# Attention value products with V's two parts in one operand, and row sums by adding DMAs, in a fused adaLN block

## The reference, cut to what matters

```python
h = layernorm(x) * (1 + cb) + sb
nx = rmsnorm(h, g1)
Q = (nx @ Wq.T).reshape(B, S, 4, 64).transpose(0, 2, 1, 3)
Kc, Vc = nx @ Wkc.T, nx @ Wvc.T                 # 64 features, one set for the 4 heads
scores = einsum('bhsd,btd->bhst', Q, Kc) / 8
out = einsum('bhst,btd->bhsd', softmax(scores), Vc)
X = h + out.transpose(0, 2, 1, 3).reshape(B, S, 256) @ Wo.T
...                                             # a shared and 8 routed experts, top 2, added to X
x = x + gb * (X + moe_out)
```

## Time and profile before

| | us |
|---|---|
| median of three runs (lowest, highest) | 1460.32 (1458.84, 1464.45) |
| profiled execution | 1461.01 |
| its span, first to last instruction | 1459.0 |
| front / loop / tail, in the span | 0 to 235 / 235 to 1114 / 1114 to 1459 |

### The profile page before, as it was taken

One profiled execution on the slowest core, in us unless ns is written; L12 is line 12 of the kernel. 1 busy time (PEld: TensorE's weight loads), 2 busy tenths in 40 slices (PEclk: granted clock), 3 DMA queues, 4 the chain that ended last, 5 costly groups with the idle time before them and its releaser, 6 DMA issues.

```text
span 1459.0 us, 19334 instructions
## 1 busy us (share of the span) xinstructions
PE 1307.4 (90%) x6008; PEld 920.7 (63%) x6008; DVE 1079.0 (74%) x2143; ACT 893.1 (61%) x1450; POOL 385.4 (26%) x282
## 2 busy tenths in 40 slices
PE   4777677999999999999998999999997999999994
PEld 2334545665666665676665666666664797887774
DVE  4956987777887777777885877787974867546778
ACT  2355564776766766666686766666675856555551
POOL 0443431222311212211111311111154001623346
PEclk9989797999999999999999999999998999999998
DMA  5001016200000000000000001000011323555634
GB/s 196 1 1 44 15 58 208 81 1 1 1 1 1 1 1 1 1 1 1 1 1 1 1 1 44 1 0 1 22 51 65 104 93 117 195 148 165 191 115 149
DMA packets 56418, 75.82 MB, mean 52 GB/s; under 512 B 8383, under 2 KB 48063, under 8 KB 56064
## 3 DMA queue, kind: packets, MB, share of 16 engines
q1 hardware_dynamic: 36030, 46.29, 9.7%
q0 software_dynamic: 6144, 16.79, 3.7%
q10 hardware_dynamic: 14146, 11.52, 2.3%
HBM read 37.27 MB, written 37.22 MB: 51 GB/s over the span
## 4 chain that ended last, share of the span: by engine, by line
PE 63%; DVE 19%; issue 5%; ACT 5%; POOL 5%; DMA 1%; ACTq 1%; POOLq 0%; DVEq 0%; SPq 0%
PE PS L1802 8%; PE PS L1700 6%; PE PS L1749 6%; PE PS L1732 6%; PE PS L1751 6%; PE PS L1735 6%; PE PS L1750 6%; DVE mx L1159 5%; PE PS L1828 4%; DVE PL L1189 4%; PE PS L1713 3%; POOL y L1534 2%; PE PS L1686 2%; POOL xbuf L1522 2%; PE PS L1786 1%
## 5 line engine op out<-in xcount | busy, mean ns | idle before, releaser
L1159 DVE TENSOR_REDUCE mx<-PS 128x1 f32<-128x512 f32 x512 | 344.1, 686 | 100.6 <-PE PS L1700 98.5
L770 ACT ACTIVATE PT<-PS 128x1024 f32<-128x1024 f32 x256 | 262.8, 1027 | 231.8 <-PE PS L1735 221.8
L1514 POOL TENSOR_TENSOR PL<-PT,PH 128x1024 fp32r<-128x1024 f32 x61 | 146.2, 2396 | 541.8 <-ACT PH L775 530.1
L775 ACT ACTIVATE PH<-PT 128x1024 fp32r<-128x1024 f32 x256 | 271.2, 1060 | 8.1
L1189 DVE TENSOR_TENSOR PL<-PT,PH 128x1024 fp32r<-128x1024 f32 x195 | 238.9, 1225 | 44.4 <-ACT PH L775 43.8
L1749 PE MATMUL PS<-PH,VH 128*65 128x512 f32 x512 | 219.6, 429 | 8.6 <-DVE PL L1189 8.6
L1751 PE MATMUL PS<-PL,VH 128*65 128x512 f32 x512 | 202.9, 396 | 0.0
L1750 PE MATMUL PS<-PH,VL 128*65 128x512 f32 x512 | 202.3, 395 | 0.0
L1700 PE MATMUL PS<-KA,Q 128*128 128x512 f32 x384 | 161.1, 432 | 16.9 <-DVE mx L1159 12.1
L1732 PE MATMUL PS<-Q,KA 128*128 128x512 f32 x384 | 128.0, 415 | 2.5 <-POOL KB L1491 2.5
L1735 PE MATMUL PS<-Q,KB 65*128 65x512 f32 x384 | 122.6, 401 | 0.0
(11 more groups left out here) (239 smaller groups left out, 2486.5 us busy)
## 6 DMA issues: line engine op xcount, KB each, us to landing
xbuf<-xT SPq DMA_DIRECT2D x26, 384.0 KB, 4.4
xg<-xbuf SPq DMA_DIRECT2D x78, 128.0 KB, 2.3
ybuf<-yo ACTq DMA_DIRECT2D x78, 128.0 KB
nxT<-in_wexp SPq DMA_DIRECT2D x9, 768.0 KB, 4.4
x<-in_x SPq DMA_DIRECT2D x8, 512.0 KB, 11.9
x_scratch<-x SPq DMA_DIRECT2D x2, 2048.0 KB, 6.9
nxT<-x_scratch SPq DMA_DIRECT2D x32, 128.0 KB
out<-X SPq DMA_DIRECT2D x32, 128.0 KB, 1.9
```

The lines of the kernel that those rows point to most:

```text
L770: act.activation(PT[:, gs % 2, :], PS[:, bk:bk + 2, :].rearrange("p a n -> p (a n)"), ACT.Exp, scale=0.125).then_inc(sem("pt"), 1)
L775: act.activation(PH[:, gs % 3, :], PT[:, gs % 2, :], ACT.Copy).then_inc(sem("pt_h"), 1)
L1159: dve.tensor_reduce(mx[:, half, i, c:c + 1], PS[:, k, :], AX, ALU.max).then_inc(sem("dve_out"), 1)
L1514: pool.tensor_tensor(PL[:, gs % 3, :], PT[:, gs % 2, :], phf[:, gs % 3, :], ALU.subtract).then_inc(sem("pl_g"), 1)
```

## The change

V's high and low part become one tile V of 2 x 64 columns. `av` makes two matmuls for each 512 queries: V (128 columns) x PH, which puts high and low part on rows 0 to 63 and 64 to 127 of the bank, and V's high part x PL on rows 0 to 63. woa has Wo on both halves of the partitions (two loads), so the projection adds the halves; it is 128x256 now. All low parts are made by VectorE.

The sum of the exponentials no longer goes through TensorE with the values. For each 1024 queries (a group g of 16 steps) two 128x1024 buffers lie in DRAM. The PT of the first two steps is written to them by SP; those of the other 14 are added by DMAs from GpSimd (`accum_op`), even steps to one buffer, odd steps to the other, each after the one before on its buffer has landed. PT has three slots, and `exp(gs)` also waits until the transfer of gs - 3 has landed. PL has two slots. When a group is through, SP reads both buffers back for 512 queries at a time (Z, 128 x 2 x 512, one slot), `z_mm` sums Z over keys with a column of ones, and VectorE takes four reciprocals at once. O holds 1024 queries only, so the projections of a head's first half are done within the head.

In the diff the first `total` and `z_mm` are SP's, the second `total` is GpSimd's (at the start of each step), the second `z_mm` TensorE's.

```diff
+        todo += spread(z_jobs(bh, 0), 61, 71) + spread(proj_jobs(bh, 0), 62, 93)
         if bh > 0:
-            m, e = (30, 60) if bh == 4 else (49, 92)
-            todo += spread(proj_jobs(bh - 1)[:8], 4, m) + spread(proj_jobs(bh - 1)[8:], m + 1, e)
+            todo += spread(z_jobs(bh - 1, 1), 13, 23) + spread(proj_jobs(bh - 1, 1), 14, 46)
...
-    last = [x for j, p in enumerate(proj_jobs(7)) for x in (p, norm[j])] + [norm[NT]]
-    side = [(-2, 9, last),
-            (2, 2, [j for ex in range(NE) for j in split_jobs(ex)]),
-            (2, 2.5, rlog_jobs(1)),
-            (22, 1, route_jobs(1, 5) + scatter_jobs(1)),
+    proj = proj_jobs(7, 1)
+    last = norm[:8] + [("z_mm", 7, 1, 0)] + proj[:4] + [("z_mm", 7, 1, 1)] + proj[4:] + norm[8:]
+    side = [(0, 9, last),
+            (4, 2.5, [j for ex in range(NE) for j in split_jobs(ex)]),
+            (4, 2.5, rlog_jobs(1)),
+            (25, 1.25, route_jobs(1, 5) + scatter_jobs(1)),
...
+    def summed(w, gs):
+        g, kc = divmod(gs, 16)
+        if kc < 2:
+            w.wait_ge(sem(f"d_zw{kc}"), 16 * (g + 1))
+        else:
+            w.wait_ge(sem(f"d_za{kc % 2}"), 16 * (7 * g + kc // 2))
...
+        def total(gs):
+            g, kc = divmod(gs, 16)
+            if kc < 2:
+                w.wait_ge(sem("pt"), gs + 1)
+                sp.dma_start(zbuf[g, kc], PT[:, gs % 3, :]).then_inc(sem(f"d_zw{kc}"), 16)
+
+        def z_mm(bh, qc, h):
+            g = 2 * bh + qc
+            if g or h:
+                pe_of(w, ("z_mm", *((bh, qc, 0) if h else (*divmod(g - 1, 2), 1)), 0))
+            for a in range(2):
+                summed(w, 16 * g + 14 + a)
+            sp.dma_start(Z[:, :, :], zbuf[g, :, :, h * 512:h * 512 + 512].rearrange("a p n -> p a n")).then_inc(
+                sem("d_z"), 32)
...
             for n in range(NTI // 3):
                 sp.dma_start(zv[n], bc(zero, 3, 1)).then_inc(sem("d_zero"), 16)
         for gs in range(NGS):
+            total(gs)
...
-            if gs >= 2:
-                low_done(w, gs - 2)
-            act.activation(PT[:, gs % 2, :], PS[:, bk:bk + 2, :].rearrange("p a n -> p (a n)"), ACT.Exp,
+            if gs >= 3:
+                w.wait_ge(sem("pl"), gs - 2)
+                summed(w, gs - 3)
+            act.activation(PT[:, gs % 3, :], PS[:, bk:bk + 2, :].rearrange("p a n -> p (a n)"), ACT.Exp,
...
-            act.activation(O[:, q0:q0 + 512], PS[0:65, 4 + n, :], ACT.Copy).then_inc(sem("o"), 1)
+            act.activation(O[:, n * 512:n * 512 + 512], PS[:, 4 + n, :], ACT.Copy).then_inc(sem("o"), 1)
...
+            dve.reciprocal(rz[:, qc, 4 * h:4 * h + 4], PS[:, k, 0:4]).then_inc(sem("dve_out"), 1)
...
-            mark(dve.reciprocal(rz[:, s, :], PS[:, k, 256:257]))
...
-            if gs >= 3:
-                w.wait_ge(sem("av"), 2 * (gs - 2))
-            dve.tensor_tensor(PL[:, gs % 3, :], PT[:, gs % 2, :], phf[:, gs % 3, :], ALU.subtract).then_inc(sem("pl_v"), 1)
+            if gs >= 2:
+                w.wait_ge(sem("av"), 2 * (gs - 1))
+            dve.tensor_tensor(PL[:, gs % 2, :], PT[:, gs % 3, :], phf[:, gs % 3, :], ALU.subtract).then_inc(sem("pl"), 1)
...
-            if not by_pool(gs):
-                low(gs)
+            low(gs)
...
-            pool.tensor_tensor(PL[:, gs % 3, :], PT[:, gs % 2, :], phf[:, gs % 3, :], ALU.subtract).then_inc(sem("pl_g"), 1)
+        def total(gs):
+            g, kc = divmod(gs, 16)
+            if kc < 2:
+                return
+            w.wait_ge(sem("pt"), gs + 1)
+            summed(w, gs - 2)
+            pool.dma_start(zbuf[g, kc % 2], PT[:, gs % 3, :], accum_op=ALU.add).then_inc(sem(f"d_za{kc % 2}"), 16)
...
+        def z_mm(bh, qc, h):
+            w.wait_ge(sem("ones"), 1)
+            w.wait_ge(sem("d_z"), 32 * (4 * bh + 2 * qc + h + 1))
+            k = bank("z_mm", bh, qc, h, 0)
+            for i in range(4):
+                for a in range(2):
+                    mm = pe.matmul(PS[:, k, i:i + 1], Z[:, a, i * P:i * P + P], ones[:, :], start=(a == 0), stop=(a == 1))
...
-            pe.matmul(PS[0:65, 4 + n, :], VH[:, t, :], PH[:, r, c], start=(kc == 0), stop=False)
-            pe.matmul(PS[0:65, 4 + n, :], VL[:, t, :], PH[:, r, c], start=False, stop=False)
-            pe.matmul(PS[0:65, 4 + n, :], VH[:, t, :], PL[:, r, c], start=False, stop=(kc == 15)).then_inc(sem("av"), 1)
+            if kc < 15:
+                pe.matmul(PS[:, 4 + n, :], V[:, t, :, :].rearrange("p a d -> p (a d)"), PH[:, gs % 3, c], start=(kc == 0),
+                          stop=False)
+                pe.matmul(PS[0:64, 4 + n, :], V[:, t, 0, :], PL[:, gs % 2, c], start=False, stop=False).then_inc(sem("av"), 1)
```

More of the change, by code:

```diff
@@ L127, in q_jobs, with proj_jobs, z_jobs @@
     return [(n, b, pair, c) for c in range(4) for n in ("q_mm", "q_hi", "q_lo")]
-def proj_jobs(bh):
-    return [("proj", bh, i) for i in range(NT)]
+def proj_jobs(bh, qc):
+    return [("proj", bh, 8 * qc + i) for i in range(8)]
+def z_jobs(bh, qc):
+    return [("z_mm", bh, qc, h) for h in range(2)]
 def norm_jobs(b):
@@ L231, in tail_order @@
     return {s: flat(v) for s, v in order.items()}
-def by_pool(gs):
-    return gs % POOL_EVERY == POOL_EVERY - 1 and gs < 7 * NSTEP + 20
-def lows(gs, pool):
-    return sum(by_pool(g) == pool for g in range(gs + 1))
 class Once:
@@ L290, in _build @@
     xbuf = [nc.dram_tensor(f"xbuf{b}", [NTI * P, D], F32, kind="Internal").ap() for b in range(NB)]
+    zbuf = nc.dram_tensor("z_scratch", [16, 2, P, 1024], F32, kind="Internal").ap()
     ybuf = [nc.dram_tensor(f"ybuf{b}", [NTI * P, D], F32, kind="Internal").ap() for b in range(NB)]
@@ L346, in _build @@
     mT = sb("mT", [8, 2, P], F32R, c=c3)
-    rz = sb("rz", [P, 2, 1], c=c3)
+    rz = sb("rz", [P, 2, 8], c=c3)
+    ones = sb("ones", [P, 1], c=c3)
     wk = sb("wk", [P, 2, P], c=c3)
@@ L394, in _build @@
     KB1 = sb("KB1", [P, S], F32R, c=c3)
-    PT = sb("PT", [P, 2, 1024], c=c3)
+    PT = sb("PT", [P, 3, 1024], c=c3)
     PH = sb("PH", [P, 3, 1024], F32R, c=c3)
-    PL = sb("PL", [P, 3, 1024], F32R, c=c3)
-    O = sb("O", [65, S], c=c3)
-    woa = sb("woa", [65, 4, 257], c=c3)
+    PL = sb("PL", [P, 2, 1024], F32R, c=c3)
+    Z = sb("Z", [P, 2, 512], c=c3)
+    O = sb("O", [P, 1024], c=c3)
+    woa = sb("woa", [P, 4, D], c=c3)
     QA = [Q01[0][:, :], Q01[1][:, :], QA2[:, :]]
@@ L616, in _ @@
         work = {"spill": spill, "max_turn": max_turn, "load_w": load_w, "split_down": split_down, "gather": gather,
-                "finish": finish}
+                "z_mm": z_mm, "finish": finish}
         run(work, FRONT)
         front_done(w)
-        sp.dma_start(woa[:, :, :], I["woA"]).then_inc(sem("d_woa"), 16)
+        for a in (0, 64):
+            sp.dma_start(woa[a:a + 64, :, :], I["woA"][0:64, :, 0:D]).then_inc(sem("d_woa"), 16)
         w.wait_ge(sem("zero"), 1)
@@ L774, in exp @@
                 w.wait_ge(sem("av"), 2 * (gs - 2))
-            act.activation(PH[:, gs % 3, :], PT[:, gs % 2, :], ACT.Copy).then_inc(sem("pt_h"), 1)
+            act.activation(PH[:, gs % 3, :], PT[:, gs % 3, :], ACT.Copy).then_inc(sem("pt_h"), 1)
         def o_out(gs, n):
@@ L1556, in _ @@
         for gs in range(NGS):
-            if by_pool(gs):
-                low(gs)
+            total(gs)
             for part in range(3):
@@ L1709, in proj, with z_mm @@
             qc, n = divmod(i, 8)
-            w.wait_ge(sem("d_woa"), 16)
+            w.wait_ge(sem("d_woa"), 32)
+            q0 = n * P
             w.wait_ge(sem("o"), 4 * bh + 2 * qc + n // 4 + 1)
             k = bank("proj", bh, i, 0)
-            pe.matmul(PS[:, k, 0:257], O[0:65, i * P:i * P + P], woa[0:65, bh % 4, :], start=True,
+            pe.matmul(PS[:, k, 0:D], O[:, q0:q0 + P], woa[:, bh % 4, :], start=True,
                       stop=True).then_inc(sem("pe_use"), 1)
+        def z_mm(bh, qc, h):
+            w.wait_ge(sem("ones"), 1)
[4 more added lines that the diff above has]
+                    mm = pe.matmul(PS[:, k, i:i + 1], Z[:, a, i * P:i * P + P], ones[:, :], start=(a == 0), stop=(a == 1))
+            mm.then_inc(sem("pe_use"), 1)
         def qk(gs):
@@ L1834, in _ @@
                 "turn_logits": turn_logits, "turn_pi": turn_pi, "oproj": oproj, "nx_turn": nx_turn, "k_mm": k_mm,
-                "v_mm": v_mm, "q_mm": q_mm, "max_mm": max_mm, "max_turn": max_turn, "proj": proj,
-                "rl_turn": rl_turn, "rl_mm": rl_mm, "count": count}
+                "v_mm": v_mm, "q_mm": q_mm, "max_mm": max_mm, "max_turn": max_turn, "z_mm": z_mm,
+                "proj": proj, "rl_turn": rl_turn, "rl_mm": rl_mm, "count": count}
         run(work, FRONT)
```

61 lines of the change are left out of this document (28 added, 33 removed), and 2 rows, old and new, of the table READERS.

## The result

| | before | after |
|---|---|---|
| median (lowest, highest), us, 4 runs each | 1460.99 (1458.84, 1464.45) | 1588.78 (1581.63, 1594.56) |
| ratio, 95% interval | | 1.087 [1.082, 1.092] |
| profiled execution, its span | 1461.01, 1459.0 | 1594.56, 1592.8 |

What follows compares the result with a forecast made beforehand. TensorE was taken to bound the loop's first 245 steps and the tail, GpSimd's scatters the last 11 steps. From 1461.0 us, -51 (loop) +20 (start) +17 (last steps) -2 (tail) = -16 gave 1445 us, range 1410 to 1510.

Steps and rivals of the forecast that it cites:

- products with ones: Row sums on TensorE (z_mm): 1.71 us each, 28 of 32 before 1074 us, 48 us of TensorE added.
- start gap: Loop start: exp(3) waits for the first write, behind the zero fills of xbuf; +20 us, bounds 10 and 27.
- The steady part: Attention loop's first 245 steps: TensorE sets the pace, 3.42 us a step falls to 3.22, a gain of 51 us.
- The tail: Experts' pipeline after the loop: fewer projections against late additions, Z reads and z_mm; -2 us, bounds -6 and +9.
- I take PE at 94.5%: 788 us, a gain of 51 us: First 245 loop steps: TensorE's remaining 745 us at a 94.5% busy share; VectorE's added low parts hidden.
- rival (b): Loop: VectorE becomes the bound with its waits unchanged, 852 us in place of 788, total 1509 us; chance 0.14.
- Rival (d): Loop: value matmuls give nothing, z_mm or LDWEIGHTS fills their place, 3.42 us a step, total 1496 us; chance 0.03.
- So I cost it at nothing: Loop's adding DMAs: 2.7 us engine time, about 4.8 us to landing, covered by TensorE's 3.22 us a step.
- rival (a): Loop: additions set the pace, 4.0 us a step, total 1636 us; decides from 3.22 us engine time; chance 0.17.
- The last 11 steps: Loop's end: twelve additions queue among the scatters on GpSimd, 58 us in place of 40; +17 us, bounds 5 and 30.
- (c): Loop: coupling costs nothing, TensorE at 97%, 768 us, scatters' stretch at its lower bound, total 1413 us; chance 0.14.
- (e): Loop: additions issued late by GpSimd, landing after 7.2 us, 3.6 us a step, total 1538 us; chance 0.05.

Runs made afterwards that it cites:

- e6: The change without transfers of PT and reads of Z (products with ones on a constant tile), every fourth low part on GpSimd as before: 1471.04 us, ratio 1.006.
- e15: Kernel before with paired value matmuls, no sums, rows scaled by a constant; slots, projections and tail order of the change: 1464.64 us, ratio 0.980.
- e16: The change without transfers of PT and reads of Z; products with ones stay, on a constant tile: 1518.31 us, ratio 1.015.
- e10: The change with its 224 additions made plain writes, same queue and waits, sums incomplete: 1532.15 us, ratio 1.050.
- e14: Kernel before with all low parts on VectorE, none on GpSimd: 1505.69 us, ratio 1.006.
- e18: Kernel before with VectorE's maximum over 256 of 512 columns, TensorE's work the same: 1459.85 us, ratio 0.976.
- e8: e16 with a third value matmul put back for each 512 queries, six a step: 1539.33 us, ratio 1.052.
- e12: The change with the tail's side jobs dealt as in the kernel before: 1565.47 us, ratio 1.074.
- e4: The change with the two sum products of a half head dealt 19 slots apart in place of 10: 1619.73 us, ratio 1.085.
- e11: The change with four chains of additions in place of two, only two buffers read back: 1570.22 us, ratio 1.075.
- e13: The change with exponentials summed in SBUF by GpSimd (VectorE in the last 12 steps), no transfers, complete output: 1688.87 us, ratio 1.157.

## Why the prediction was wrong

**By parts**, as differences of the ratios to the kernel before, 14.6 us for each per cent: pairs alone 0.980 (-30 us, of which the tail's order is +20), products with ones +2.7% (+39, e6 against e15), low parts +0.9% (+13, e16 against e6), transfers as plain writes +3.5% (+51, e10 against e16, of which 24 are the start gap), additions in place of plain writes +3.7% (+55, the change against e10). The sum is the measured +128 by the way it is made, since each part starts from the kernel of the part before; it checks nothing. The low parts came out as 9 us in e14 and 13 here, and the parts cross chips, so each is good to some 5 us.

By stretch the forecast missed in two places. The steady part was to give 51 us and cost 71. The tail was to give 2 and cost 22. The steady part's 122 us divide where the transfers begin: without them (e16) it takes 840.5 us, some 13 more than before in place of 51 less, which is 64 us of the miss; with them 898.4, 58 more in place of nothing.

**Value matmuls and low parts: the step that failed first** is "I take PE at 94.5%: 788 us, a gain of 51 us". I took a busy share as a measure of how much of a step is TensorE's to give, and one stretch of 34 us as proof that VectorE's load doesn't matter. e18 shows that VectorE's reads of the maxima were in the loop's pace before the change, and e15 that 112 us of matmuls were worth 44 to 52. A busy time of 96% holds records of 0.39 us at a pitch of 0.23, so small waits between matmuls stay covered by the record of the one before: the steady part of before shows 30 us of idle time and has 94 us beyond the pitch. Without transfers the steady part took 840.5 us (e16, 241 steps) against 839.3 in e14 on the same chip, which has all low parts on VectorE too: pairs and products with ones cancel, and what the low parts cost stays. That is nearest to rival (b), which had VectorE bound and gave +13 us; it had 0.14. That the number fits so well is luck in part: (b) kept VectorE's wait for the maxima at 97 us, and it was 62.6 in e16. Rival (d), that nothing comes of the value matmuls because z_mm fills their place, had the steady part at no gain and 0.03; that is near too as a sum, but e8 and e15 put the value matmuls at 44 to 55 us and not at nothing. The price of the products with ones was near (48 us of TensorE; 39 us of time; 16 records in 1.84 us where v_mm had 1.89), that of the low parts, taken as hidden, was 9 to 13 us.

**The adding DMAs: the other step that failed**, by 58 us in the steady part, is "So I cost it at nothing". I took 2.7 us of engine time and 4.8 us to landing; it was 3.23 and 5.7. The bounds of 1.33 and 4.0 held it, and a plain write at 1.30 was as read from the earlier trace rows. The Trainium skill (Collectives: The Full Stack, The bandwidth ceiling) has half the rate of a copy for the adding step of a ring of cores. An estimate by that rule from e10's 1.30 would be 2.6 us; the trace has 2.5 times the copy, and the measurement decides. With 14 additions, two plain writes and two reads of Z in 16 steps, the DMA work of a step is (14 x 3.23 + 4 x 1.30) / 16 = 3.15 us against a step of 3.73. So rival (a) was at the point that it named (3.22), yet the pace was not set by the queue alone: the exponentials wait for landings only 65.6 us. What the time follows is the load of the DMA engines: 4% busy in the steady part and 840.5 us (e16), 44% and 847.4 (e10), 87% and 889.8 (e12). What I had not asked is what an engine set does to the transfers beside it when it is that busy. Three things differ between the change and e10 from 268 us to exp(244). The first line is the change's, the other two are e10's:

```profile
PE PS L1745 <- DMA Z<-z_scratch: 14.7, 8, 3.5
PE PS L1745 <- DMA Z<-z_scratch: 0.2, 1, 0.2
...
ACT PT L788 <- DMA z_scratch<-PT: 34.3, 5, 25.6
```

TensorE waits 14.5 us more for Z. The exponentials wait 31 us more for landings (65.6 and 34.3, or 39.7 and 8.7 without the wait at the start). The granted clock is 0.93 and not 0.96 (0.97 in e16, 0.99 before). The first two are not the price by themselves: e4 took the waits for Z away and e11 those for landings, and neither brought the steady part down by more than 5 us. For the clock there is an estimate from above, with its two levels at 0.5 and 1: 0.93 over 897 us is about 126 us at the lower level, 0.96 over 846 us about 68. If TensorE worked all through them they cost half of that, 63 and 34, so about 29 of the 51 us at most. How the 51 us divide, and why the clock falls more often, stays open; that late transfers stop TensorE and the matmuls behind them run slower is seen in single places, such as the one in head 3, and not shown as the sum.

**The start gap** was right in its cause: predicted +20, measured +24, ended by the landing of the first write, which SP issued at 262.58 behind the zero fills. In the size I misread a row: 246.01 us is the start of exp(4), and exp(3) began at 242.97. From there to my 266 us is 23 us, and exp(3) began at 267.26; the 2 us to be caught up and the slower restart, which I had set against each other, can't be told from this. Before, and after:

```profile
242.97 1.03 ACT L770 ACTIVATE PT<-PS 128x1024 f32<-128x1024 f32 x1 [1.42 <-PE PS L1735]
...
267.26 1.02 ACT L788 ACTIVATE PT<-PS 128x1024 f32<-128x1024 f32 x1 [25.95 <-DMA z_scratch<-PT]
```

**The last 11 steps** were right in the number: 53.3 us, +16.4 where +17 was said, with the scatters and additions in one line on GpSimd. The mechanism was right in part, and the close fit is luck in part. In the chain of waits it was not issue time alone; additions that had to land stood in it as well:

```profile
1209.15 5.46 DMA z_scratch<-PT
...
1214.80 1.00 POOL xbuf L1547
```

**The tail** failed in sign: -2 was said with bounds -6 and +9, and it was +22. The chain there:

```profile
1228.04 7.73 DMA z_scratch<-PT
...
1235.85 3.41 DMA Z<-z_scratch
...
1239.30 3.57 PE PS L1745 x16
```

The last addition lands 16.8 us after the start of the last exponential, Z another 3.5 us later, and the product takes 3.57 us at the lower clock (granted 0.57 in the 25 us had at 0.86), twice the 1.84 of the loop. I had said that TensorE has shared tiles to do meanwhile; the order put the norms in one block and the splits two tiles later. e12 gives back 21 of the 22 us with all transfers in place, so the order was the price and the late Z alone was not. Which of its changes held the tail up is not separated.

Of the lines that should show it wrong, "ACT's exponentials waiting for DMA all through the loop" did not come, and TensorE's waits for L1159's successor did (78.9 us for weight loads alone), over the 60 named for (b); without transfers they were there as well (73.7 in e16, and 38.2 in the kernel before). Of the other rivals, (c) needed the pairs at full worth. (e) did not come: GpSimd's issue of an addition takes 884 ns on average and 1212 at most, and the additions land in 5.7 us (median), under its 6.4. Of the lines that should show the forecast right, the additions under 6 us came (as a median) and GpSimd's unbroken last steps in part, although the forecast was wrong: they tested its smaller terms.

## What to carry to other kernels

A busy share near 100% on TensorE does not say that removing matmuls pays: shorten the partner's work first (one edit, here the reduce over half of the columns) and see whether the time moves, because a matmul taken away from a place where TensorE would have waited anyway wins nothing. Moving a reduction from a spare row of a matmul into DRAM is not free because the DMA engines were idle: count engine time per step with the addition at 2.5 plain copies, and keep it well below the step (here 44% busy cost 7 us in the steady part, less than the same kernel differs between chips, and 87% about 50). The one kernel with all its sums that beat both is e18, which has nothing of the change in it; its shift of the softmax leaves half of the keys out, so it holds only where their scores don't exceed the others' by much.

## What was not expected of the hardware

- An adding DMA of 512 KB from SBUF to DRAM takes 3.23 us of all 16 engines and 5.7 us to landing, a plain one 1.30 and 2.9 (e10); its issue on GpSimd is 0.88 us.
- Two-input elementwise work on GpSimd slows VectorE's two-input work (e13): 1974 ns for a subtraction that overlaps a GpSimd addition, 1217 for one that doesn't. VectorE's reduce from PSUM beside it stays at 683. GpSimd's own 128x1024 addition takes 2697 where its subtraction took 2396 in the kernel before, on every fourth step.
- DMA engines 87% busy slow no instruction of VectorE or ScalarE: the subtraction has 1220 ns in the kernel after and 1225 in the one before, the exponential 1024 and 1027.
